# A TensorE transpose of 128 x 128 made as two transposes of 64 pixels, on two row halves of the array, in a deformable convolution block

## The chip, the cores and the metric

The kernel runs on one core of one Trainium2 chip. The metric is the device time of one execution in microseconds (us). Two per cent, about 2.06 us here, is roughly what a measurement of this kernel can tell from no change.

## The reference, cut to what matters

Four images of 256 channels and 16 x 16 pixels go through two blocks. The first block reduces to 64 channels, normalises, and then samples each pixel at nine places (taps) that a small convolution has computed, with bilinear weights and a mask; the samples are multiplied by the weights `w2` and summed. Normalisation, a 1 x 1 convolution to 256 channels and a residual follow. The second block is a chain of quantised convolutions.

```python
v = jnp.take_along_axis(xf, idx, axis=2).reshape(B, C, *Ksp)      # one corner of bilinear_sample
w = (wy * wx * valid).astype(x.dtype)[:, None]
...
sampled = bilinear_sample(out, py, px) * mask[:, None]
out = jnp.einsum('bckhw,ock->bohw', sampled, w2.reshape(w2.shape[0], w2.shape[1], K))
out = jax.nn.relu(group_norm(out, gn2_scale, gn2_bias))
out = conv(out, w3)
```

## The kernel before, in words

The four images are two pairs: `b2` (0 or 1) is the place in the free dimension, `h` (0 or 1) the half of the partitions. A pixel's sample is a product with a sparse matrix. For one output pixel, one tap and all 16 x 16 input pixels the weights are an outer product of a row vector and a column vector of 16 "hat" values. The kernel makes them for 128 output pixels at a time, with the output pixels on the partitions: `make_g(i)` (L872 to L880, on VectorE) writes `g_rows[i % 3]`, 128 partitions x (9 taps x 256 input pixels), for i = 0 to 7. The hat values come from `make_hats` and, for t = 1 to 3, from GpSimd (L341, L344). `make_g(i)` waits from i = 3 on for the turn i - 3, whose buffer it takes.

TensorE contracts over partitions, so the weights have to be turned: input pixels on the partitions, output pixels in the free dimension. The first six (`BY_PE` = 6) are turned by TensorE: `turn(i)` (L455 to L470) makes 9 taps x 2 halves of the input pixels = 18 transposes of 128 x 128 in float32, six of them in each of three PSUM slots of two banks, and after each slot's last one adds one to `turned`. ScalarE's `copy_g(i)` (L702 to L711) evicts a slot, 128 partitions x 768 elements, in one instruction (L709) into `g_cols` or `g_last`, and adds one to `g_copied`. The last two (i = 6 and 7) go another way: VectorE turns blocks of 32 x 32 (L914), SyncE's and GpSimd's queues place them with 16 DMAs (`place_blocks`, L292 to L299) into `g_placed`.

The order on TensorE around the change is written out by hand. It is: the products `v` with `w2` (L433, L439: 64 rows of the array each, the two image halves on rows 0 to 63 and 64 to 127); turns 0 to 4; `sample(0, 0, 2)`; turn 5; `sample(0, 3, 8)` (L479), which ends the samples of pair 0; parts of `sample_half(3, ...)` (L495, on `g_last`) with `pair_sums` and `conv3(0)` (L512) between them; and then `sample_half(2, ...)` (L495, on `g_placed`), which waits for the 16 DMAs. After it come `pair_sums(5, 1)` and the normalisation of pair 1, and then the second block. ScalarE's and VectorE's `norm3` also wait for the 16 DMAs, since `y0` lies over `g_blocks`. `idle(n, bank)` issues matmuls of zeros (L359), whose results nobody reads.

Of the kernel before, what the change touches and what calls it, by code (L numbers as in the profile page):

```python
# [38 lines left out]
P = 128  # L39
B, C, H, W = 4, 256, 16, 16  # L40
HALVES = 2
B2 = B // HALVES
N = H * W
CB = 64
# [5 lines left out]
NQ = N // P  # L50
T = B2 * NQ
ROWS_Q = H // NQ
PER_SLOT = 3
# [3 lines left out]
BANK = 512  # L57
# [43 lines left out]
def build(nc, x, first, pairs, consts, woff, grid, w2, w3, wq, out):  # L101
    with ExitStack() as ctx:
        def sb(name, shape, dt=F32):
            return ctx.enter_context(nc.sbuf_tensor(name, shape, dt))

        def ps(name, shape):
            return ctx.enter_context(nc.psum_tensor(name, shape, F32))
# [12 lines left out]
        ident = consts_sb[:, C_ID:C_ID + P]  # L120
# [21 lines left out]
        g_rows = [sb(f"g_rows{i}", [P, TAPS, H, W]) for i in range(3)]  # L142
# [58 lines left out]
        slot = [ps(f"slot{i}", [P, 2 * BANK]) for i in range(3)]  # L201
# [76 lines left out]
        def rows(h):  # L278
            return slice(CB * h, CB * h + CB)
# [75 lines left out]
        def _(pe):  # L355
# [35 lines left out]
            def om_step(b2, s):  # L391
                for p in range(2):
                    k = s + TAPS_A * p
                    if k < TAPS:
                        mm = nc.tensor.matmul(slot[0][CB * p:CB * p + CB, BANK * b2:BANK * b2 + N],  # L395
                                              woff_sb[:, k, :], window(feat, b2, k), start=(s == 0),
                                              stop=(k in (TAPS_A - 1, TAPS - 1)))
                return mm
# [12 lines left out]
            for b2 in range(B2):  # L411
                pe.wait_ge(feat_ready, b2 + 1)
                for s in range(TAPS_A):
                    mm = om_step(b2, s)
# [21 lines left out]
            def make_last_v(i):  # L436
                b2, q, h = i // 4, i // 2 % 2, i % 2
                at = BANK * h + CB * (i // 2)
                return nc.tensor.matmul(slot[0][:, at:at + CB], feat_flat[rows(h), N * b2 + P * q:N * b2 + P * q + P],  # L439
                                        w2_sb[rows(h), BANK:TAPS * CB], start=True, stop=True)  # L440
# [6 lines left out]
            for i in range(2, 2 * T):  # L447
                make_v(i)
                mm = make_last_v(i)
# [3 lines left out]
            slot_of = (1, 2, 0)  # L453

            def turn(i):  # L455

                pe.wait_ge(g_ready, i + 1)
                for j in range(TURNS):
                    if i == 0:

                        pe.wait_ge(v_ready, (1, 6, 2 * T + 1)[j])
                    else:

                        pe.wait_ge(g_copied, TURNS * (i - 1) + j + 1)
                    for k in range(PER_SLOT * j, PER_SLOT * j + PER_SLOT):
                        for q in range(NQ):
                            at = P * (NQ * (k - PER_SLOT * j) + q)
                            mm = nc.tensor.transpose(slot[slot_of[j]][:, at:at + P],  # L468
                                                     g_rows[i % 3][:, k, ROWS_Q * q:ROWS_Q * q + ROWS_Q, :], ident)
                    mm.then_inc(turned, 1)  # L470

            def sample(b2, first_tap, last_tap):
# [28 lines left out]
            for i in range(5):  # L501
                turn(i)
            sample(0, 0, 2)
            turn(5)
            sample(0, 3, 8).then_inc(sampled, 1)

# [70 lines left out]
            for b2 in range(B2):  # L577
                for part, ready in ((n1_lo, lo_ready), (n1_hi, hi_ready)):
                    if part is n1_hi or b2 == 1:
                        idle(IDLE[14 + (part is n1_hi) + 2 * b2 - 1], spare)  # L580
                    for c in range(CH):
                        pe.wait_ge(ready, CH * b2 + c + 1)
                        for h in range(HALVES):
                            mm = nc.tensor.matmul(acc[b2][rows(h), 0:N], wqb[:, Q_W1 + CB * c:Q_W1 + CB * c + CB],
                                                  part[:, c, b2, h, :], start=(part is n1_lo and c == 0),
                                                  stop=(part is n1_hi and c == CH - 1))
# [41 lines left out]
        def _(a):  # L628
# [73 lines left out]
            def copy_g(i):  # L702

                t, h = ORDER[i] // HALVES, ORDER[i] % HALVES
                for j in range(TURNS):
                    a.wait_ge(turned, TURNS * i + j + 1)
                    per = PER_SLOT * NQ
                    dst = g_cols[h][:, :, t, :] if t < NQ else g_last[h][:]
                    nc.scalar.activation(dst[:, per * j:per * j + per, :],  # L709
                                         slot[(1, 2, 0)[j]][:, 0:per * P].rearrange("p (k n) -> p k n", k=per),  # L710
                                         ACT.Copy).then_inc(g_copied, 1)  # L711

            for i in range(BY_PE):
                copy_g(i)
                if i == 4:
                    a.wait_ge(wq_in, 16)
                    nc.scalar.activation(wq_sign[:], wq_sb[:], ACT.Sign).then_inc(sign_ready, 1)
                    nc.scalar.activation(wq_mag[:], wq_sb[:], ACT.Abs).then_inc(sign_ready, 1)
# [72 lines left out]
            for i, (c, b2, h, n) in enumerate(PIECES):  # L791
                a.wait_ge(sum_ready, 4 * B2 + i + 1)
                if i == len(PIECES) - 1:
                    n = 1
# [390 lines left out]
```

## Time and profile before

| | us |
|---|---|
| median of three runs | 102.83 |
| lowest and highest run | 102.51 and 106.87 |
| span of the profiled execution | 101.5 |
| TensorE busy, weight loads busy | 80.3, 54.1 |
| VectorE, ScalarE, GpSimd busy | 70.7, 48.5, 24.0 |

The span goes from the first to the last instruction of one execution. The page gives no separate time for the profiled execution beyond its span; the span is 1.3 us under the median of the runs and 1.0 us under the lowest. Shares of busy time say little here, since the engines work in turns along one chain; the order of events between 28 and 64 us is what matters.

### The profile page before, as it was taken

Reading aid. Unit: us, or ns where it says so; the run is one execution under the profiler, and the core shown is the slowest. Engines: PE = TensorE matmul, PEld = TensorE weight load, DVE = VectorE, ACT = ScalarE, POOL = GpSimd, SP = SyncE. Lnnn points to the kernel's source line nnn. Section 1 sums busy time; section 2 is a strip of 40 time slices with the busy share of each in tenths; the row PEclk is TensorE's granted clock in tenths of the full one; section 3 lists DMA queues with packets and bytes.
Section 4 is the critical chain, followed back from the end, with each engine's and each line's share of the span. In section 5 each row is a group of like instructions: output and inputs, shape, how many; then the busy total and the mean of one; then the engine's idle time right before and its main releaser. Section 6 shows DMA issues by size and latency. Waiting matters only on the chain.

```text
span 101.5 us, 1692 instructions
## 1 busy us (share of the span) xinstructions
PE 80.3 (79%) x638; PEld 54.1 (53%) x642; DVE 70.7 (70%) x181; ACT 48.5 (48%) x87; POOL 24.0 (24%) x21
## 2 busy tenths in 40 slices
PE   5999999975986159999999699999836959598400
PEld 2335656644876158586698389656422528284100
DVE  1225397997993599999559604388589795857970
ACT  5003465959997506969112003340457254453770
POOL 7401104899999300004300400000000000000000
PEclk9999999999999985999999999999999999999995
DMA  2999200000000000005999500000000000000056
GB/s 46 311 356 362 98 0 0 0 6 0 0 0 0 0 0 6 3 0 144 233 249 212 100 0 3 6 0 0 0 0 0 0 0 0 0 6 3 0 183 230
DMA packets 4040, 6.49 MB, mean 64 GB/s; under 512 B 512, under 2 KB 2944, under 8 KB 4032
## 3 DMA queue, kind: packets, MB, share of 16 engines
q1 hardware_dynamic: 3568, 5.53, 18.8%
q0 software_dynamic: 192, 0.59, 2.4%
q10 hardware_dynamic: 272, 0.26, 0.8%
q8 instruction: 5, 0.08, 0.4%
q14 instruction: 3, 0.02, 0.1%
HBM read 2.98 MB, written 1.05 MB: 40 GB/s over the span
## 4 chain that ended last, share of the span: by engine, by line
PE 33%; DVE 24%; POOL 17%; issue 7%; SPq 6%; ACT 5%; DMA 5%; DVEq 0%; POOLq 0%; ACTq 0%
POOL hats L341 11%; DVE g_rows L879 6%; SPq L297 6%; POOL hats L344 6%; PE slot L359 6%; DMA g_placed<-g_blocks 5%; PE slot L395 5%; PE acc L605 5%; PE acc L495 4%; DVE g_blocks L914 3%; PE acc L370 3%; DVE g_cols L1011 3%; ACT g_cols L796 3%; PE slot L512 2%; ACT pad L765 2%
## 5 line engine op out<-in xcount | busy, mean ns | idle before, releaser
L879 DVE TENSOR_TENSOR g_rows<-hats 128x2304 f32<-128x2304 f32 x8 | 21.0, 2668 | 3.9 <-POOL hats L344 3.9
L468 PE MATMUL slot<-consts_sb,g_rows 128*128 128x128 f32 x108 | 15.0, 296 | 6.3 <-DVE g_rows L879 4.4
L468 PEld LDWEIGHTS slot<-consts_sb,g_rows 128*128 128x128 f32 x108 | 13.0, 151 | 8.1 <-DVE g_rows L879 5.1
L359 PE MATMUL slot<-zeros 128*128 128x512 bf16 x49 | 14.1, 417 | 1.5 <-DVE zeros L815 1.2
L341 POOL TENSOR_SCALAR hats<-hats 128x576 f32<-128x576 f32 x3 | 10.9, 3626 | 0.3 <-ACT hats L672 0.3
L709 ACT ACTIVATE g_cols<-slot 128x768 f32<-128x768 f32 x12 | 8.8, 844 | 0.9 <-PE slot L468 0.9
L359 PEld LDWEIGHTS slot<-zeros 128*128 128x128 bf16 x53 | 5.2, 107 | 7.2 <-issue 2.9
L479 PE MATMUL acc<-g_cols,v_sb 128*64 128x256 f32 x72 | 8.3, 385 | 0.0
L709 ACT ACTIVATE g_last<-slot 128x768 f32<-128x768 f32 x6 | 4.6, 812 | 5.4 <-PE slot L468 5.4
L344 POOL TENSOR_TENSOR hats<-hats,mask 128x288 f32<-128x288 f32 x4 | 5.9, 1477 | 4.7 <-DVE hats L870 4.4
L479 PEld LDWEIGHTS acc<-g_cols,v_sb 128*64 128x64 f32 x72 | 5.1, 141 | 2.9 <-ACT g_last L709 0.3
L638 ACT ACTIVATE std<-var,eps_sb 128x1 f32<-128x1 f32 x4 | 1.2, 294 | 10.5 <-DVE var L830 10.5
L765 ACT ACTIVATE pad<-g_cols 64x256 bf16<-64x256 int8 x8 | 3.3, 418 | 4.8 <-DVE g_cols L1011 4.7
L495 PE MATMUL acc<-g_placed,v_sb 128*64 128x128 f32 x72 | 4.6, 277 | 1.3 <-DMA g_placed<-g_blocks 1.3
L297 POOL DMA_DIRECT2D g_placed<-g_blocks x4 | 2.2, 553 | 14.0 <-DVE g_blocks L914 14.0
L914 DVE STREAM_TRANSPOSE g_blocks<-g_rows 128x576 f32<-128x576 f32 x8 | 5.4, 740 | 0.0
L824 DVE BATCH_NORM_STATS2 stats<-acc 128x6 f32<-128x256 f32 x4 | 1.7, 430 | 4.8 <-PE acc L370 2.7
L395 PE MATMUL slot<-feat,woff_sb 128*64 128x256 f32 x36 | 4.7, 385 | 0.0
L495 PEld LDWEIGHTS acc<-g_placed,v_sb 128*64 128x64 f32 x72 | 3.9, 137 | 1.5 <-DMA g_placed<-g_blocks 1.5
L746 ACT ACTIVATE dev_sb<-slot 128x4 f32<-128x4 f32 x2 | 0.3, 173 | 8.9 <-PE slot L522 8.9
L495 PE MATMUL acc<-g_last,v_sb 128*64 128x128 f32 x72 | 4.5, 275 | 0.0
L495 PEld LDWEIGHTS acc<-g_last,v_sb 128*64 128x64 f32 x72 | 4.0, 137 | 0.5 <-issue 0.3
(128 smaller groups left out, 145.1 us busy)
## 6 DMA issues: line engine op xcount, KB each, us to landing
g_placed<-g_blocks SPq DMA_DIRECT2D x12, 144.0 KB, 4.7
out<-g_cols SPq DMA_DIRECT2D x4, 256.0 KB, 2.3
x_sb<-x SPq DMA_DIRECT2D x3, 256.0 KB, 3.9
g_placed<-g_blocks POOLq DMA_DIRECT2D x4, 144.0 KB, 4.7
wq_sb<-wq SPq DMA_DIRECT2D x1, 484.5 KB, 5.7
woff_sb<-woff SPq DMA_DIRECT2D x1, 288.0 KB, 4.9
w_sb<-w SPq DMA_DIRECT2D x1, 288.0 KB, 4.9
x_sb<-x ACTq DMA_DIRECT2D x1, 256.0 KB, 2.9
```

The source lines that it names most:

```text
L297: queue.dma_start(g_placed[BLOCK * j:BLOCK * j + BLOCK, i].rearrange("p h k n -> p (h k n)"), g_blocks[BLOCK * i:BLOCK * i + BLOCK, j].rea ...
L341: nc.gpsimd.tensor_scalar(v, v, 1.0, 1.0, ALU.min, ALU.subtract).then_inc(hats_cut, 1)
L344: nc.gpsimd.tensor_tensor(hats[:, t, :, 1], hats[:, t, :, 1], mask[:, t // NQ, t % NQ].unsqueeze(3).to_broadcast([P, HALVES, TAPS, H]), AL ...
L359: nc.tensor.matmul(bank, zeros[:, 0:P], zeros[:], start=True, stop=True)
L395: mm = nc.tensor.matmul(slot[0][CB * p:CB * p + CB, BANK * b2:BANK * b2 + N], woff_sb[:, k, :], window(feat, b2, k), start=(s == 0), stop= ...
L468: mm = nc.tensor.transpose(slot[slot_of[j]][:, at:at + P], g_rows[i % 3][:, k, ROWS_Q * q:ROWS_Q * q + ROWS_Q, :], ident)
L479: mm = nc.tensor.matmul(acc[b2][rows(h), 0:N], v_sb[:, B2 * h + b2, q, k, :], g_cols[h][:, NQ * k + q].rearrange("p a n -> p (a n)"), star ...
L495: mm = nc.tensor.matmul(acc[1][rows(h), at:at + P], v_sb[:, B2 * h + 1, q, k, :], g_last[h][:, NQ * k + q, :] if t % NQ == 1 else g_placed ...
L709: nc.scalar.activation(dst[:, per * j:per * j + per, :], slot[(1, 2, 0)[j]][:, 0:per * P].rearrange("p (k n) -> p k n", k=per), ACT.Copy). ...
L765: nc.scalar.activation(dst, src, ACT.Copy, scale=256.0).then_inc(hi_ready, 1)
L879: tt(g_rows[i % 3][:], hats[:, t, h, 1].unsqueeze(3).to_broadcast([P, TAPS, H, W]), hats[:, t, h, 0].unsqueeze(2).to_broadcast([P, TAPS, H ...
L914: nc.vector.transpose(g_blocks[:, j, h], g[:, :, j, :]).then_inc(blocks_turned, 1)
```

## The change

Each transpose of 128 partitions (output pixels) x 128 (input pixels) becomes two. The one with r = 0 takes partitions 0 to 63 and the one with r = 1 partitions 64 to 127; each loads its 64 x 128 piece as weights and moves a 64 x 64 identity, so that it writes 128 partitions x 64 columns. The results of r = 0 go to the first bank of the slot and those of r = 1 to the second. `rows(r)` is the slice of 64 partitions. A slot still holds three taps, 384 columns in each bank where there were 768 columns in a row, and it is still evicted by one instruction, which now reads both banks in runs of 64 and writes them interleaved, so that the tile in SBUF is as before. The numbers of semaphore updates and waits are the same.

```diff
@@ turn(i), TensorE
                         for q in range(NQ):
-                            at = P * (NQ * (k - PER_SLOT * j) + q)
-                            mm = nc.tensor.transpose(slot[slot_of[j]][:, at:at + P],
-                                                     g_rows[i % 3][:, k, ROWS_Q * q:ROWS_Q * q + ROWS_Q, :], ident)
+                            at = CB * (NQ * (k - PER_SLOT * j) + q)
+                            for r in range(HALVES):
+                                mm = nc.tensor.transpose(
+                                    slot[slot_of[j]][:, BANK * r + at:BANK * r + at + CB],
+                                    g_rows[i % 3][rows(r), k, ROWS_Q * q:ROWS_Q * q + ROWS_Q, :],
+                                    ident[rows(r), CB * r:CB * r + CB])
                     mm.then_inc(turned, 1)
@@ copy_g(i), ScalarE
                     dst = g_cols[h][:, :, t, :] if t < NQ else g_last[h][:]
-                    nc.scalar.activation(dst[:, per * j:per * j + per, :],
-                                         slot[(1, 2, 0)[j]][:, 0:per * P].rearrange("p (k n) -> p k n", k=per),
+                    src = slot[(1, 2, 0)[j]][:].rearrange("p (r n) -> p r n", r=HALVES)[:, :, 0:per * CB]
+                    nc.scalar.activation(dst[:, per * j:per * j + per, :].rearrange("p k (r n) -> p k r n", r=HALVES),
+                                         src.rearrange("p r (k n) -> p k r n", k=per),
                                          ACT.Copy).then_inc(g_copied, 1)
```

## Rows read from the trace of the kernel before

**Rows 1.** Chain that ended last, in order of time: start us, us, what

```profile
28.83 4.42 POOL hats L341
...
41.44 2.56 DVE g_rows L879
...
44.03 3.43 DVE g_blocks L914 x5
47.46 0.54 SPq L297
...
53.82 4.72 DMA g_placed<-g_blocks
...
58.59 1.09 PE acc L495 x16
...
61.79 2.33 PE acc L495 x40
```

**Rows 2.** Timeline of the turns: start us, us, engine, line, xcount, [idle before <-releaser]

```profile
28.35 2.19 PE L468 MATMUL slot<-consts_sb,g_rows 128*128 128x128 f32 x18 [0.44 <-DVE g_rows L879]
...
34.03 9.96 DVE L879 TENSOR_TENSOR g_rows<-hats 128x2304 f32<-128x2304 f32 x4 [2.79 <-POOL hats L344]
...
36.64 3.69 PE L468 MATMUL slot<-consts_sb,g_rows 128*128 128x128 f32 x18 [3.16 <-DVE g_rows L879]
...
40.26 2.93 PE L479 MATMUL acc<-g_cols,v_sb 128*64 128x256 f32 x24
...
43.12 2.18 PE L468 MATMUL slot<-consts_sb,g_rows 128*128 128x128 f32 x18
44.03 2.22 ACT L709 ACTIVATE g_last<-slot 128x768 f32<-128x768 f32 x3 [1.05 <-PE slot L468]
```

**Rows 3.** Timeline from the end of sample(0) to the wait for the blocks

```profile
50.68 0.43 DVE L824 BATCH_NORM_STATS2 stats<-acc 128x6 f32<-128x256 f32 x1 [1.26 <-PE acc L479]
...
53.27 0.56 ACT L643 ACTIVATE feat<-acc,gn_bias,gn_scale 128x256 f32<-128x256 f32 x1 [0.56 <-DVE gn_bias L839]
...
54.32 1.99 PE L512 MATMUL slot<-feat,w_sb 128*128 128x256 f32 x8
...
56.24 1.09 PE L495 MATMUL acc<-g_last,v_sb 128*64 128x128 f32 x16
...
58.59 1.09 PE L495 MATMUL acc<-g_placed,v_sb 128*64 128x128 f32 x16 [1.26 <-DMA g_placed<-g_blocks]
```

**Rows 4.** Instructions of L433 and of L439: ns min/median/max, first and last start

```profile
L433 PE MATMUL slot<-w_sb,feat_flat x8: 589/617/693, 15.2 to 19.2; 64*128 64x512 f32 x8
...
L439 PE MATMUL slot<-w_sb,feat_flat x16: 216/272/320, 16.9 to 21.1; 64*128 64x64 f32 x16
```

**Rows 5.** Weight loads by form: xcount, busy us, mean ns of one, idle before

```profile
L468 PEld LDWEIGHTS slot<-consts_sb,g_rows 128*128 128x128 f32 x108 | 13.0, 151 | 8.1 <-DVE g_rows L879 5.1 <-ACT v_sb L697 1.5 <-ACT v_sb L679 0.9
...
L439 PEld LDWEIGHTS slot<-w_sb,feat_flat 64*128 64x128 f32 x16 | 2.0, 186 | 1.1 <-issue 1.0
...
L406 PEld LDWEIGHTS slot<-consts_sb,om_sb 128*128 128x128 f32 x8 | 1.0, 190 | 1.1 <-DVE om_sb L854 0.8 <-issue 0.4
```

**Rows 6.** Timeline of TensorE's loads at 13.18 us, of L406

```profile
13.18 0.52 PEld L406 LDWEIGHTS slot<-consts_sb,om_sb 128*128 128x128 f32 x4 [0.38 <-issue]
```

**Rows 7.** Timeline of TensorE at 15.21 us, two products v on two row halves

```profile
15.21 0.30 PEld L433 LDWEIGHTS slot<-w_sb,feat_flat 64*128 64x128 f32 x4 [0.39 <-issue]
...
15.21 1.13 PE L433 MATMUL slot<-w_sb,feat_flat 64*128 64x512 f32 x4
```

**Rows 8.** Busy by stretch: length, PE (x) PEld (x) DVE ACT POOL, granted clock, DMA, GB/s

```profile
30.29:33.70 3.41, 2.43 (x21) 1.96 (x19) 0.95 (x1) 2.68 (x5) 3.33 (x2) 1.00 0.00 0
33.71:37.12 3.41, 0.48 (x4) 0.48 (x5) 3.09 (x2) 0.72 (x2) 0.29 (x1) 1.00 0.00 0
37.12:40.53 3.41, 3.41 (x18) 3.08 (x18) 3.41 (x2) 1.79 (x3) 0.00 (x0) 0.50 0.02 5
...
84.00:85.00 1.00, 1.00 (x21) 0.85 (x18) 0.65 (x4) 0.07 (x2) 0.00 (x0) 1.00 0.00 0
```

## The prediction

> **What bounds the kernel now.** I read first the chain of work that ended last, then the timeline of TensorE, VectorE and ScalarE over the turns, then the waits before the samples of the last image half.
>
> The chain [rows 1] passes by the turns altogether. GpSimd's hat values end at about 34.0 us, VectorE makes its last four outer products one after the other from 34.03 to 43.99 us [rows 2], then turns blocks of 32 x 32 from 44.03 us, SyncE issues DMAs up to 53.82 us, the last lands at 58.55 us, and TensorE starts `sample_half(2, ...)` at 58.59 us. No row of L468 or L709 is in it. The reader is to see three distances in the timeline:
>
> - Does VectorE wait for a turn? It makes i = 4 to 7 in 9.96 us without a break [rows 2], that is 2.49 us each, so i = 7 starts at 41.50 us at the latest (41.44 us in the chain [rows 1]). It needs turn 4's end, which is 36.64 + 3.69 = 40.33 us [rows 2]. The slack is 1.1 us.
> - Does TensorE reach the blocks late? It is idle for 1.26 us before 58.59 us, and the DMA is named as what ended it [rows 3]. All turns and all samples on `g_cols` and `g_last` lie before that wait.
> - Is ScalarE late? Before its evictions of turn 5 it sat idle for 1.05 us, waiting for TensorE [rows 2].
>
> So TensorE's turns lie beside a chain of hats, outer products, block transposes, DMA issues and landing, with 1.1 and 1.26 us to spare. After 58.59 us TensorE is on the chain, but no turn is left by then.
>
> **What a turn costs, and what the change makes of it.** A turn of 18 transposes takes 2.19 us, its last result's way out included [rows 2]. Is that the columns moved or the load? With 64 columns moved a float32 matmul takes at least 216 ns, with 512 at least 589 ns [rows 4]: 373 ns for 448 columns, 0.83 ns a column, so 128 columns are 107 ns, and 18 x 107 = 1.92 us. With the last one's 0.2 to 0.3 us of latency that is the 2.19 us. So the moved columns set the pace and the loads are hidden.
>
> Removed and added: per turn 18 matmuls of 128 columns and 18 loads become 36 matmuls of 64 columns and 36 loads.
>
> *Columns moved*: 64 x 0.83 = 53 ns for a half.
>
> *Loads*: rows make no difference (186 ns for 64 x 128, 190 ns for 128 x 128 [rows 5]). The four loads of L406 took 0.52 us [rows 6], so (0.52 - 0.19) / 3 = 0.11 us apart, where only 64 columns were moved: there the load set the pace. A transpose's load has a mean of 151 ns instead of 190 [rows 5], so I put its pace 40 to 50 ns lower, at 60 to 70 ns. A half then costs 53 ns by columns or about 60 ns by loads.
>
> *Do the halves run beside each other?* The nearest rows are the products `v`: 64 rows of the array each, the two image halves on the two row halves, into two banks. Four matmuls of 512 columns (427 ns each by the price above) took 1.13 us [rows 7]; one after the other they would take 4 x 427 = 1.71 us and the latency. With a load of 0.1 us, two rounds of 427 ns and 0.17 us of latency the sum is 1.13 us: two at a time. Their four loads took 0.30 us [rows 7] where four in a row take 0.52 us [rows 6]: the loads overlap too. In contrast the eight matmuls of 256 columns on all rows took 1.99 us [rows 3], 8 x 213 = 1.71 us and latency: one at a time. So I take full overlap: 18 x 60 ns = 1.1 us a turn.
>
> *Bounds.* From below 18 x 53 = 0.95 us. From above three steps. By issue: the densest second of this trace has 21 matmuls and 18 loads in 1.00 us [rows 8], 26 ns an instruction; 72 instructions would be 1.85 us. One after the other with hidden loads: 36 x 60 = 2.15 us. Each half as dear as a whole, 107 ns: 36 x 107 = 3.85 us. I take 1.1 us, because rows 7 show the same layout of rows and banks, and keep up to 3.85 us for the rivals.
>
> First the row, then the rule: loads of 64 and of 128 rows took 186 and 190 ns [rows 5]. The Trainium skill, page "TensorE: Matmul & The Clock Gate", Part 2, says the same, that a load's time goes by its columns and not by its rows, which speaks against this change: it doubles the loads. The page gives 128 columns / 1.2 GHz, an estimate of 107 ns each, or 3.84 us for 36 in a row, against 1.1 us by my rows; its Part 3 adds that a load overlaps a matmul in flight when the row group differs, and that is the case here. The first rule alone leads to the third rival.
>
> *Eviction.* The same 768 elements a partition, three in 2.22 us [rows 2], 740 ns each. It now reads two banks in runs of 64 instead of one run of 768. No row shows runs of 64 across two banks. At nothing the rate stays; twice as dear would be 1.5 us an eviction, 4.4 us a turn. That is no likely size, since the outputs to `g_cols` are already in runs of 128 and to `g_last` contiguous at no visible difference; I take nothing, at most 0.1 us each, which ScalarE's idle 1.05 us covers.
>
> *Waits, queues, semaphores*: the numbers of updates and waits stay. Nothing is queued differently on SyncE, GpSimd or VectorE. Nothing to pay.
>
> **The sum.** On the chain: zero instructions removed, zero added, so 101.5 us of span stays 101.5 us. Beside it: turn 4 now ends at about 38.2 to 38.8 us instead of 40.33 us (half of it at the low clock, below), `sample(0, 0, 2)` at about 41.9, turn 5 at 43.0, and `sample(0, 3, 8)` ends near 48.4 instead of 50.5 us. What is late next: VectorE is turning blocks until 49.4 us, so the statistics start 1.2 us sooner, at 49.5 instead of 50.68 us [rows 3]; `conv3(0)` follows at 53.0 instead of 54.32 us; the last of `sample_half(3)` ends at about 55.9 instead of 57.33 us. Then TensorE waits for the DMAs until 58.55 us as before: the idle time grows from 1.26 to some 2.7 us, and that is where the gain goes. ScalarE's and VectorE's `norm3` wait for the same DMAs. The time stays at the median, 102.8 us; the profiled span is 1.3 us below the median and I keep that distance.
>
> **Rivals.**
>
> *1. The halves do not run beside each other* (the change does not do what it says). For: no transpose on row halves is in the trace. Against: rows 7. The turn is then 1.85 to 2.15 us instead of 2.19: TensorE comes to its wait at most where it does now. 102.8 us. A chance of 0.12.
>
> *2. The longer idle time lowers the clock.* In 33.71 to 37.12 us TensorE worked for only 0.48 us, waiting for VectorE, and in the next stretch the granted clock was 0.50, 1.2 GHz; before, with 2.43 us of turns in 3.41 us, it was 1.00, 2.4 GHz [rows 8]. Shorter turns leave more idle time in 28 to 37 us, where a lower clock costs nothing on the chain (turn 4 ran mostly at the low clock already), but also before 58.59 us, where TensorE is the chain from then on. If the clock is low for a stretch like that one, work of 3.41 us at the low clock is worth 1.7 us at the high one: up to +1.7 us, 104.5 us; if it touches only a part, about +1.0 us, 103.8 us. Against: the idle time of 2.7 us is shorter than the 3.16 us before 36.64 us [rows 2], and there is work around it. A chance of 0.10. The Trainium skill, page "TensorE: Matmul & The Clock Gate", Part 4, says that transposes do not raise the clock; by that rule turns 2 and 3 would not have held it, but the trace shows 1.00 through 30.29 to 33.70 us, with only turns in it.
>
> *3. Slower: each half costs as much as a whole*, because load and matmul of neighbouring halves exclude each other. Turn 3.85 us instead of 1.96. It decides as soon as turns 4 and 5 together lengthen by more than the slack of 1.26 us. Turns 0 to 3 run on without a pause (turn 1 from 26.2, turn 2 from 30.1, turn 3 from 34.0 us), turn 4 ends at 41.8 us instead of 40.33, VectorE's i = 7 starts 0.4 us late. Then 2.9 us of samples, turn 5 to 48.5 us, samples to 53.8 us instead of 50.5: 3.3 us late, less 1.26 us of slack, +2.1 to +2.4 us: 104.9 to 105.2 us. Against: rows 7, where loads of two row halves overlap. A chance of 0.06.
>
> **How the numbers follow.** Forecast 0.70 (102.8 us, 102.3 to 103.2 by the scatter of runs: 102.51 and 102.83 us), rival 1 0.12, rival 2 0.10, rival 3 0.06, and 0.02 for a gain of over 2% by a way that I do not see. The predicted time is the forecast's, 102.8 us. The range takes in the forecast, rival 1 and most of rival 2: 102.1 to 104.4 us. The low end allows 0.7 us, since the chip of the next runs may be another. Two per cent is 2.06 us: faster 0.02, slower 0.08 (rival 3, and the far end of rival 2 with a little scatter), the same 0.90.
>
> **What would show it.** L468 with 216 matmuls and 216 loads; 36 of them in 1.1 to 1.3 us where 18 took 2.19 us at the high clock (1.85 to 2.15 us is rival 1, 3.85 us rival 3). The eviction within 0.1 us of before. The first DMA wait of L495 ending at 58.5 us after the start, with an idle time of 2.5 us or more instead of 1.26 us, and the chain still going by L344, L879, L914, L297. The granted clock before and after 58.6 us tells rival 2. The prediction is wrong if a turn is longer than about 2.6 us, or if the landing of the blocks moves.

## The result, and the profile after

The changed kernel took 107.21 us (median of 4 runs, 106.51 to 107.97) against 103.11 us of the kernel before (102.51 to 106.87, 4 runs). The ratio is 1.0378, with a 95% interval of 1.0307 to 1.0449: slower. One thing is needed to read all numbers below: the kernel before has executions of about 103 us and others of 104.5 to 106.9 us, the ratios leave out those that lie over 1.5% above the fastest of their kernel, and the medians do not.

The forecast was 102.8 us. The profiled execution has a span of 104.7 us instead of 101.5 us.

The chain that ended last, after (start us, us, what), answers to [rows 1]:

```profile
38.28 5.03 DVE g_rows L883 x2
...
43.33 5.41 DVE g_blocks L918 x8
48.74 0.82 SPq L297
...
52.74 5.96 DMA g_placed<-g_blocks
...
58.74 1.97 PE acc L498 x16
```

The chain goes by the same work, and TensorE starts on the placed blocks at 58.74 us, where it was 58.59 us. Up to there only 0.15 us is lost, the sum of two parts: GpSimd's hat values ended at 33.3 us instead of 34.0 us and with them VectorE's block transposes at 48.7 us instead of 49.4 us, and the blocks landed 10.0 us after that instead of 9.1 us (8.8 to 9.3 us in the other profiled executions with placed blocks). What comes next costs more: the 16 matmuls that took 1.09 us now take 1.97 us, and the whole stretch to the variance of pair 1 is longer. Before that point the timeline of TensorE, after, answers to [rows 2, 3]:

```profile
27.66 2.19 PE L469 MATMUL slot<-consts_sb,g_rows 64*128 64x64 f32 x36 [0.42 <-DVE g_rows L883]
...
35.95 2.19 PE L469 MATMUL slot<-consts_sb,g_rows 64*128 64x64 f32 x36 [3.16 <-DVE g_rows L883]
...
38.06 4.55 PE L482 MATMUL acc<-g_cols,v_sb 128*64 128x256 f32 x24
...
42.55 1.34 PE L469 MATMUL slot<-consts_sb,g_rows 64*128 64x64 f32 x36
43.17 2.21 ACT L713 ACTIVATE g_last<-slot 128x768 f32<-128x768 f32 x3 [2.27 <-PE slot L469]
...
54.82 1.09 PE L498 MATMUL acc<-g_last,v_sb 128*64 128x128 f32 x16
...
58.74 1.97 PE L498 MATMUL acc<-g_placed,v_sb 128*64 128x128 f32 x16 [2.83 <-DMA g_placed<-g_blocks]
```

The same 36 halves took 2.19 us at 27.66 us and 1.34 us at 42.55 us: the first at 1.2 GHz, the second at 2.4 GHz, as the next view shows. Three evictions still take 2.21 us. TensorE now stands idle for 2.83 us before the blocks, where it was 1.26 us. Busy time by stretch, after (length, PE, PEld, DVE, ACT, POOL, granted clock, DMA share, GB/s), answers to [rows 8]:

```profile
24.57:41.62 17.05, 12.61 (x170) 10.25 (x168) 14.25 (x6) 12.26 (x17) 8.56 (x4) 0.50 0.01 1
41.63:58.69 17.06, 14.29 (x178) 10.85 (x174) 12.71 (x27) 5.34 (x7) 3.36 (x5) 1.00 0.63 140
58.70:65.52 6.82, 6.77 (x50) 6.08 (x52) 0.74 (x5) 0.44 (x2) 0.00 (x0) 0.50 0.00 0
```

There are two stretches at 0.50, 1.2 GHz. The first, 24.57 to 41.62 us, lies beside VectorE's chain. The second, 58.70 to 65.52 us, begins where TensorE becomes the chain: 6.82 us at half the clock hold work of 3.4 us, and the span grew by 104.7 - 101.5 = 3.2 us. The kernel before had 1.00 there.

### The profile page after: what moved, and what is told of

It reads as the page before. It is cut to its first block, busy times and chain, and to the rows that moved or that the text cites. A ratio compares the mean times of both kernels' runs of the same rounds, so it can differ in the third digit from the quotient of the medians.

```text
span 104.7 us, 1912 instructions
## 1 busy us (share of the span) xinstructions
PE 81.3 (78%) x750; PEld 54.8 (52%) x750; DVE 70.6 (67%) x181; ACT 48.3 (46%) x87; POOL 24.0 (23%) x21
## 4 chain that ended last, share of the span: by engine, by line
PE 30%; DVE 26%; POOL 16%; DMA 10%; SPq 5%; issue 5%; ACT 4%; DVEq 0%; POOLq 0%; ACTq 0%
POOL hats L341 10%; DVE g_rows L883 7%; PE acc L498 6%; DMA g_placed<-g_blocks 6%; POOL hats L344 6%; DVE g_blocks L918 5%; DMA x_sb<-x 4%; PE slot L395 4%; PE acc L608 4%; SPq L297 4%; PE slot L359 3%; DVE g_cols L1015 3%; PE slot L515 2%; ACT g_cols L800 2%; ACT pad L769 2%
## 5 line engine op out<-in xcount | busy, mean ns | idle before, releaser
L469 PE MATMUL slot<-consts_sb,g_rows 64*128 64x64 f32 x216 | 12.4, 287 | 7.1 <-DVE g_rows L883 4.3
L359 PE MATMUL slot<-zeros 128*128 128x512 bf16 x53 | 14.6, 411 | 1.2 <-DVE zeros L819 1.2
L469 PEld LDWEIGHTS slot<-consts_sb,g_rows 64*128 64x128 f32 x216 | 11.0, 193 | 8.5 <-DVE g_rows L883 4.9
L482 PE MATMUL acc<-g_cols,v_sb 128*64 128x256 f32 x72 | 10.0, 440 | 0.0
L498 PE MATMUL acc<-g_placed,v_sb 128*64 128x128 f32 x72 | 6.9, 361 | 2.8 <-DMA g_placed<-g_blocks 2.8
L482 PEld LDWEIGHTS acc<-g_cols,v_sb 128*64 128x64 f32 x72 | 5.8, 160 | 3.4 <-issue 1.5
L498 PEld LDWEIGHTS acc<-g_placed,v_sb 128*64 128x64 f32 x72 | 5.8, 189 | 3.1 <-DMA g_placed<-g_blocks 3.1
```

Source lines behind the costliest of these rows:

```text
L359: nc.tensor.matmul(bank, zeros[:, 0:P], zeros[:], start=True, stop=True)
L469: mm = nc.tensor.transpose(slot[slot_of[j]][:, BANK * r + at:BANK * r + at + CB], g_rows[i % 3][rows(r), k, ROWS_Q * q:ROWS_Q * q + ROWS_Q ...
L482: mm = nc.tensor.matmul(acc[b2][rows(h), 0:N], v_sb[:, B2 * h + b2, q, k, :], g_cols[h][:, NQ * k + q].rearrange("p a n -> p (a n)"), star ...
L498: mm = nc.tensor.matmul(acc[1][rows(h), at:at + P], v_sb[:, B2 * h + 1, q, k, :], g_last[h][:, NQ * k + q, :] if t % NQ == 1 else g_placed ...
```

## The experiments

Two theories went in. A: the longer pause before the blocks lets the clock fall for the work behind it. B: something else behind 58.7 us became slower, a DMA or an eviction. Kernels of one group below ran on one chip, beside the kernel before.

**1. a_fill8: bridge the pause.**

```diff
             sample_half(3, 7, 8)
+            idle(8, spare)
             sample_half(2, 0, 1)
```

> The changed kernel with eight matmuls of zeros (L359, about 0.21 us each, 1.7 us in all) between the last part of sample_half(3) and the wait for the placed blocks, in the second bank of slot 1, where nothing else lies at that time. Theory A (the longer idle time before the blocks lets TensorE's clock fall to 1.2 GHz for the work behind them, which is the chain): the granted clock stays 1.00 from 58.7 us on, the 3.2 us come back, and the time is within 1% of the kernel before, about 103 us. Theory B (the landing of the blocks or something behind it is slower for another reason, a DMA or an eviction): 106 to 107.5 us as in the changed kernel.

It took 103.44 us (103.01 to 103.49), ratio 0.9912 (0.9848 to 0.9976) to the kernel before, whose runs in this group are at 103.33 to 104.89 us: the same within two per cent. The changed kernel was not run in this group; its ten runs in two others are all at 105.29 us or above. The blocks in its timeline:

```profile
58.81 1.09 PE L498 MATMUL acc<-g_placed,v_sb 128*64 128x128 f32 x16 [0.93 <-DMA g_placed<-g_blocks]
```

The start is the same, the 16 matmuls are back at 1.09 us, and so are some 3 us of the time. Theory B would have left them where they were.

**2. b_less: lengthen the pause in the kernel before, with less work.**

```diff
             conv3(0)
-            sample_half(3, 7, 8)
             sample_half(2, 0, 1)
```

The last image half lacks taps 7 and 8.

> The kernel before without sample_half(3, 7, 8), so that the last image half lacks two of nine taps: 1.1 us less work on TensorE, and an idle time before the blocks of 2.4 us instead of 1.26 us. Theory A: the clock falls behind the idle time and the kernel with less work is slower by 1.5 to 3.3 us, 104.5 to 106 us, at least in some of its executions. Theory B: nothing changes or a little is gained, 102.5 to 103.1 us.

Its four runs are 102.93, 103.41, 106.64 and 106.86 us. The profiled one is the last of them, with a mean granted clock of 0.943. By stretch:

```profile
55.60:59.01 3.41, 0.00 (x0) 0.00 (x0) 1.03 (x6) 0.00 (x0) 0.41 (x1) 1.00 0.57 112
59.02:65.83 6.81, 6.75 (x50) 6.05 (x52) 0.73 (x5) 0.44 (x2) 0.00 (x0) 0.50 0.00 0
```

With whole transposes, a pause of 3.70 us in this execution, and less work, TensorE falls to 1.2 GHz at the same place and for as long as in the changed kernel. Two runs of four, 102.93 and 103.41 us, show no loss of time. No low stretch lies before this fall, so the halves and the low clock around them are not needed for it. Together with a_fill8, where the halves stand and only the pause is shorter, this puts the cost on the pause and not on the halves as such. How often a longer pause leads to a fall is not told by four runs, two of them high, since the kernel before has high runs too.

**3. b_fill4: shorten the pause in the kernel before.** `idle(4, spare)` at the same place.

> The kernel before with four matmuls of zeros (0.85 us) in its idle time of 1.26 us before the blocks. Theory A: the clock is 1.00 there already in the profiled execution, so its time stays 102.5 to 103; if the scatter of the kernel before (102.5 to 106.9 us) comes from the same clock, its upper runs disappear. Theory B: no change, and the scatter stays.

Its four runs are 103.01 to 103.30 us, ratio 0.9896 (0.9834 to 0.9959); the seven runs of the kernel before on this chip lie at 103.33 to 104.89 us, five of them at 104.48 or above with a mean clock of 0.942 to 0.943. The scatter of the kernel before disappears with most of the pause (0.34 us is left in the profiled execution). That fits a kernel at the edge of the same loss; none of its high runs was profiled. With both pauses bridged the two kernels stand at 103.44 and 103.21 us: the change alone is worth nothing that these runs can tell.

**4. a_serial: the order of the halves.**

```diff
+                    for r in range(HALVES):
                         for k in range(PER_SLOT * j, PER_SLOT * j + PER_SLOT):
                             for q in range(NQ):
                                 at = CB * (NQ * (k - PER_SLOT * j) + q)
-                                for r in range(HALVES):
                                 mm = nc.tensor.transpose(
```

> The changed kernel with the same 216 half transposes in another order: in each slot first the six of the upper row half, then the six of the lower one, so that neighbours are on the same rows. If it is the order that lets two halves run beside each other, a turn at the full clock takes 36 x 60 = 2.1 us and the latency instead of 1.34 us. Theory A in its narrow form (only the shortened turns, by the longer idle time, lower the clock): TensorE comes to the blocks as late as before, the clock stays up at 58.7 us, 103 us. In its wider form (halves on 64 rows count as less work for the clock, so that it is low from 24 us on): turns take about 4 us, TensorE is late for the blocks by up to 3 us, and the time is 104 to 107 us. Theory B: 106 to 107.5 us.

Its runs are 102.47, 104.84, 106.48 and 106.79 us. The profiled one is the fastest:

```profile
43.31 1.52 PE L469 MATMUL slot<-consts_sb,g_rows 64*128 64x64 f32 x36
...
57.80 1.09 PE L498 MATMUL acc<-g_placed,v_sb 128*64 128x128 f32 x16 [0.94 <-DMA g_placed<-g_blocks]
```

```profile
25.63:29.04 3.41, 3.26 (x52) 3.08 (x50) 3.41 (x2) 2.97 (x5) 3.33 (x3) 0.50 0.00 0
29.05:42.68 13.63, 10.25 (x114) 8.04 (x113) 10.85 (x5) 8.44 (x11) 4.37 (x2) 0.50 0.01 2
```

Two things are in it. First, a turn with neighbours on the same rows takes 1.52 us, not 2.1 us and latency: my expectation was wrong, and so was the reason that I gave for the short turn. Second, 52 halves kept TensorE busy for 3.26 of 3.41 us at the low clock, and the clock did not rise, whereas in the kernel before the whole transposes of turn 4, a later place, kept it busy for all of 37.12 to 40.53 us at the low clock and were followed by the full one [rows 8]. Which difference between the two decides was not tried. Here the low clock from 25.63 to 42.68 us cost nothing: with a start on the blocks at 57.80 us this is the shortest span of the kernels with placed blocks profiled here, 100.7 us. The blocks also landed sooner in it, 8.8 us after VectorE's last block transpose instead of 9.1 us.

The other three runs, 104.84 to 106.79 us, were not profiled. A pause of 0.94 us in one execution says nothing of theirs, and the trial does not decide between the theories: the profiled run is near the 103 us of theory A in its narrow form, two others are in the range of theory B. For the profiled one the wider form of A is ruled out, since TensorE was ready before the blocks.

**5. a_fillall: keep the clock up around the turns too.** 24 more matmuls of zeros: 3 before each of turn 0's first two slots, 2 after turn 1, 6 after turn 2, 10 after turn 3.

> The changed kernel with the eight matmuls of zeros before the blocks as in a_fill8, and 24 more in TensorE's pauses around the turns (3 each before the first two slots of turn 0, 2 after turn 1, 6 after turn 2, 10 after turn 3), which should keep the clock up from 24 to 42 us too. Theory A (only the clock behind 58.6 us costs anything, since the turns lie beside the chain through VectorE and the DMAs): the first low stretch disappears, TensorE is ready about 2 us earlier, and the time is that of a_fill8, 103.0 to 103.5 us, or, if eight matmuls are no longer enough to bridge the longer pause, up to 106.5 us. Theory C (the low clock in 24 to 42 us costs time as well): 101.5 to 102.5 us.

The granted clock is 1.00 from 5 to 95 us, and the time is 103.94 us (103.25 to 104.09, 10 runs), ratio 1.0055 (1.0006 to 1.0104). The median is 0.4 us above the range that I gave for theory A; four runs lie at 103.25 to 103.39 us and six at 103.91 to 104.09 us, and why was not followed up. Turn 4 took 1.34 us and TensorE reached the pause early, to wait for the blocks as before:

```profile
58.62 1.09 PE L500 MATMUL acc<-g_placed,v_sb 128*64 128x128 f32 x16 [0.99 <-DMA g_placed<-g_blocks]
```

So the low clock of 24 to 42 us is not what slowed the changed kernel: without it the time is no better than that of a_fill8, which has it.

**6. v8_half, v8_whole, v8_bare: take the bound away.** All eight outer products are turned by TensorE; VectorE's block transposes and the 16 DMAs are gone, and with them the pause. `g_third` is a pair of tiles like `g_last`.

```diff
-BY_PE = 6
+BY_PE = 8
...
             sample(0, 0, 2)
             turn(5)
-            sample(0, 3, 8).then_inc(sampled, 1)
+            sample(0, 3, 5)
+            turn(6)
+            sample(0, 6, 6)
+            turn(7)
+            sample(0, 7, 8).then_inc(sampled, 1)
```

v8_half has the halves and the 24 matmuls of zeros of experiment 5, v8_whole the whole transposes and the same matmuls of zeros, v8_bare the halves without them. The lines above show only the number and the order of the turns; in all three the quantisation of the weights on ScalarE and VectorE also stands elsewhere.

> The bound taken away: all eight outer products are turned by TensorE (turns 6 and 7 between the samples of pair 0), VectorE's 32 x 32 transposes and the 16 DMAs are gone, and the same 24 matmuls of zeros keep the clock up; halves as in the changed kernel. Two smaller moves go with it: the weights' quantisation on ScalarE and VectorE stands where these engines are now idle. Theory A says that the change's gain was hidden by the blocks: sample_half(2) starts at about 56.6 us instead of 58.6 us, and the time is 100.5 to 102 us. If something else binds (ScalarE with 24 evictions of 0.74 us, or the statistics), 102.5 to 104 us.

> The same as v8_half with the whole 128 x 128 transposes of the kernel before. A turn is 0.84 us longer (2.18 against 1.34 us at the full clock), and four of them (4 to 7) stand in TensorE's way now. Theory A: 2.5 to 3.5 us slower than v8_half, 103.5 to 105.5 us. If the halves gave nothing even where the turns bind, the same as v8_half.

> v8_half without the 24 matmuls of zeros. Here the turns and samples from 24 to 42 us are on TensorE's path to sample_half(2), so if halves let the clock fall there, as in the changed kernel (24.6 to 41.6 us at 1.2 GHz), turn 4 and the first samples take some 2 to 3 us more: 1.5 to 3 us slower than v8_half. If the clock stays up, the same as v8_half.

| | median, range us | ratio to the kernel before |
|---|---|---|
| v8_half | 101.30, 101.00 to 102.27 | 0.9843 (0.9744 to 0.9942) |
| v8_whole | 104.66, 104.03 to 104.69 | 1.0133 (1.0040 to 1.0226) |
| v8_bare | 103.09, 101.85 to 104.34 | 0.9952 (0.9893 to 1.0010) |

The timeline of v8_half, turns 5 and 6 and the first samples on `g_third`:

```profile
39.81 1.33 PE L455 MATMUL slot<-consts_sb,g_rows 64*128 64x64 f32 x36
...
43.85 1.90 PE L455 MATMUL slot<-consts_sb,g_rows 64*128 64x64 f32 x36
...
56.45 1.04 PE L481 MATMUL acc<-g_third,v_sb 128*64 128x128 f32 x16
```

And of v8_whole, turn 5 and the same samples:

```profile
41.58 2.19 PE L454 MATMUL slot<-consts_sb,g_rows 128*128 128x128 f32 x18
...
60.16 1.04 PE L478 MATMUL acc<-g_third,v_sb 128*64 128x128 f32 x16
```

Where the turns are on the path, the halves give 104.66 - 101.30 = 3.4 us, as four turns at 0.85 us each would; the starts on `g_third`, 56.45 and 60.16 us, show that it has come in by then. v8_half is 1.6% under the kernel before, and the interval excludes equal times but not a gain of less than two per cent. v8_whole, with the same other edits, is 1.3% above it, so the other edits alone do not give the gain. v8_bare is 1.8 us slower than v8_half. Its samples on `g_third` start at 58.70 us instead of 56.45 us, since here the low clock around the turns lies on the path:

```profile
24.88:41.93 17.05, 12.65 (x164) 10.29 (x166) 14.26 (x6) 12.94 (x17) 8.17 (x4) 0.50 0.01 2
```

**7. a_again: the two kernels' shares.** The changed kernel once more.

> The changed kernel once more, unchanged, to set the shares of executions side by side: the kernel before has executions with a mean clock of about 0.97 (102.5 to 103.9 us), of 0.942 (104.5 to 105.1 us) and of 0.93 (106.0 to 106.8 us). Theory A: in the changed kernel the pause before the blocks is 2.8 us instead of 1.26 us, so nearly all executions lose the clock behind 58.6 us: 8 of 10 or more above 104.4 us. If the first result was chance, the two kernels have the same shares.

Six runs of the changed kernel: 105.29 to 108.09 us, median 106.47, none with a mean clock above 0.894. The profiled one has a pause of 2.76 us and again a low stretch of 6.82 us, but it begins later:

```profile
60.14:66.96 6.82, 6.82 (x60) 6.36 (x59) 1.28 (x6) 1.91 (x5) 0.00 (x0) 0.50 0.00 1
```

TensorE started on the blocks at 58.48 us at 1.00 and had worked for 1.66 us when the clock fell. The fall comes at the end of the pause in one execution and shortly behind it in the other.

The kernel before, 21 runs on this chip: seven at 102.62 to 103.66 us and fourteen at 104.83 to 106.72 us, median 105.09. The ratio is 1.0269 (1.0162 to 1.0376), slower with an interval that reaches below two per cent; that of the medians is 1.013, since the kernel before is at 104.83 us or above in two of three executions here, probably by part of the same loss. The mean clock does not tell its executions apart, as my expectation had it: three of 102.62 to 103.50 us have 0.926 or 0.927, less than any of the fourteen from 104.83 us on.

**8. a_fill4: half the bridge.** `idle(4, spare)` instead of eight.

> The changed kernel with four instead of eight matmuls of zeros before the blocks, so that the pause is about 2.0 us, between the 0.9 us of a_fill8 and the 2.83 us of the changed kernel. Theory A: some executions keep the clock and some lose it, or all keep it: between 103.0 and 106.5 us, more scatter than a_fill8. Theory B, by which the pause does not matter: 106 to 108 us.

Ten runs: six at 102.80 to 103.70 us and four at 104.64, 106.07, 107.02 and 107.04 us; the ratio to the kernel before is 1.0022 (0.9968 to 1.0076). The pause in the profiled execution, of the first kind, is 1.68 us. With half the bridge some executions lose time and some do not, with the whole bridge (0.93 us of pause in the profiled execution) none of four, and without it (2.83 and 2.76 us) all ten runs of the changed kernel lie at 105.29 us or above. The pauses of the executions that were not profiled are not known.

**9. v8_serial: the order of the halves, where it counts.**

> v8_half with the order of the halves of a_serial (six of the upper row half, then six of the lower one). In a_serial's trace a turn took 1.52 us at the full clock instead of 1.34 us, so neighbours on the same rows cost only 0.18 us a turn. Four turns stand on TensorE's path: 0.7 us slower than v8_half, 101.7 to 102.2 us. If the running side by side of the two row halves were what makes the turn short, as the prediction said (2.1 us a turn otherwise), it would be 3 us slower, about 104.3 us.

It took 102.36 us (102.00 to 104.31), ratio 0.9905 (0.9857 to 0.9952), beside 101.30 us and 0.9843 for v8_half in another group, on another chip; the profiled spans are 100.3 and 99.2 us. A turn is 1.51 us here. The order is worth 0.17 us a turn, 0.7 us in four of them; the difference of 0.6 to 1.1 us between the two groups fits that and can't be read more closely. The order is not where most of the shorter turn comes from.

## Why the prediction was wrong

**What bounds the kernel.** Right. The chain through hats, outer products, block transposes, DMA issues and landing is the same, and TensorE starts on the blocks at 58.74 us.

**The step that failed: the work behind the blocks, taken as unchanged, and rival 2 with it.** The sum put nothing on the chain, so that the span would stay at 101.5 us. Only rival 2 touched TensorE's work behind 58.59 us. Its mechanism is what happened, and both its price and its chance were off. I priced it at "up to +1.7 us", from the one low stretch in the trace of before. The low stretch behind the pause lasts 6.82 us, twice that, and costs 3.2 to 3.4 us; I had taken the length of one example for the length of all. And I gave it 0.10, with the argument that the pause was shorter than the 3.16 us before 36.64 us and had work around it; all ten runs of the changed kernel lie at 105.29 us or above, and both profiled ones have the fall. The trace of before had only one pause with a fall behind it, and one of 1.26 us without, and says nothing of where between them the edge is; a run of 106.87 us among three, which I had seen, was a sign that the edge might be near, since a_fill8, b_fill4 and a_fill4 tie that scatter to the pause. The range of 102.1 to 104.4 us followed from these two errors.

**The cost of a turn.** The size was nearly right, 1.34 us for the 1.1 us and latency that I took, and the reason was not. I ascribed the gain to two halves running beside each other and priced a half alone at 60 ns. The last load's own 0.14 us taken off, 36 loads in 1.38 us (a_serial) are 35 ns apart and in 1.20 us (after) 30 ns apart. Most of the gain is in the half transpose itself, a third of the 107 ns of a whole one; my price of a half by columns, 53 ns, was too high too (35 ns with neighbours on the same rows), and the pace of 60 to 70 ns that I put on a load was twice too high. Why a half is so cheap, no run separates. The bound by issue, 1.85 us a turn from 26 ns an instruction, was no bound: 72 instructions passed in 1.34 us. The rule of the Trainium skill on loads ("TensorE: Matmul & The Clock Gate", Part 2) gave an estimate of 107 ns a load in a row; by a_serial, with neighbours on the same rows, a load and its matmul took 35 ns, and the measurement decides.

**Eviction and waits.** Right: three evictions 2.21 us instead of 2.22 us.

**Where the gain goes.** Right as to place: the gain ends in the pause before the blocks. That the numbers meet so closely, the last of `sample_half(3)` ending at 55.91 us (forecast 55.9) and a pause of 2.83 us (forecast 2.7), is partly luck. The low clock had begun at 24.57 us, so turn 5 ended at 43.89 us (forecast 43.0) and the samples of pair 0 at 49.21 us (forecast 48.4); VectorE, which was to set the start of the statistics, was ready 0.7 us sooner than in the profile of before and waited 0.53 us for TensorE; and the blocks took 0.8 us longer to land. In a_again, where they took only 0.1 us longer, the pause is 2.76 us.

The rule of the Trainium skill that transposes do not raise the clock ("TensorE: Matmul & The Clock Gate", Part 4) fails for whole transposes, by [rows 8]. The halves of a_serial left the clock at 0.50, as the rule has it, but so did the plain matmuls of the changed kernel from 58.70 us on, so that this does not bear the rule out.

**Rivals 1 and 3.** The turn of rival 1 (1.85 to 2.15 us, no running side by side) did not occur. How far two halves do run beside each other is not settled, since even neighbours on the same rows make a turn of 1.52 us. Rival 3 (3.85 us a turn) is ruled out. The slowing came from the opposite of rival 3: TensorE was too early, not too late.

**Left open.** Whether all of the executions of the kernel before at 104.5 to 106.8 us lose the clock at this pause: none of them was profiled; that b_fill4 had none in four runs speaks for it. Two of the first four runs of the changed kernel, 107.80 and 107.97 us, are 1.3 us above the profiled one, and the fall that was profiled does not account for this. What makes a low stretch end was not tried.

## What to carry to other kernels

A faster step beside the chain lengthens the pause in front of the next wait, and TensorE's clock may fall to half at the end of that pause or shortly behind it, exactly where TensorE becomes the chain. Look at the granted clock behind each wait that a change lengthens, and try to bridge it with matmuls of zeros, which was enough here. Price such a fall by the whole low stretch behind it, here 6.82 us, and not by the pause. One high run among three was a sign here that the kernel might be at the edge already. A gain hidden behind a bound is worth having once the bound is moved: the halves gave nothing that the runs can tell beside the DMAs, and 3.4 us where TensorE turned everything.

## What the runs showed of the hardware

- A float32 transpose of 64 rows x 128 columns, moving 64 columns, went at 30 to 35 ns in a row (36 in 1.34 and 1.52 us with latency), one of 128 x 128 moving 128 columns at 107 ns (18 in 2.18 us). A half turns half of the data and cost a third of the time.
- At a granted clock of 0.50 the halves kept TensorE busy for 3.26 of 3.41 us and the clock did not rise (a_serial, 25.63 to 29.04 us); whole transposes that kept it busy for 3.41 of 3.41 us were followed by a rise (kernel before, 37.12 to 40.53 us). In the changed kernel it was low from 24.57 us on, where the kernel before had 1.00 up to 37.12 us; with 24 matmuls of zeros in the pauses around the same halves (a_fillall) it was 1.00 throughout.
- After a pause of 2.83 us the clock was low for 6.82 us although TensorE was busy for 6.77 us of it. After one of 2.76 us (a_again) TensorE worked at 1.00 for 1.66 us, and then the clock was low for 6.82 us with TensorE busy all the time.
